# The third routing moved into the merged stage, and the second weights scaled by GpSimd in the second mixture

## The chip, the cores and the metric

The kernel runs on one core of one Trainium2 chip. The metric is the device time of one execution in microseconds, as the median of several runs. A profile of one execution (the trace) shows every instruction of the engines: TensorE (PE; its weight loads as PEld), VectorE (DVE), ScalarE (ACT), GpSimd (POOL) and the queue of SyncE (SP), which issues the DMAs.

## What is computed

`x` has 32 tiles of 128 tokens with 128 features; a context `ctx` has the same shape. Four layers follow each other, each of them a cross-attention onto the context and a feed-forward network, both added to `x` through a tanh gate. The networks are mixtures of 8 experts of which each token uses 2. What matters here is the network of the third layer and the attention of the fourth:

```python
# third network, N = 4096 tokens in all (the reference's shapes follow x)
capacity = int(1.2 * (N // E + 1))
logits = xf @ router_w.T + router_b
probs = softmax(logits)
top_vals, top_inds = top_k(probs, 2)
top_vals = top_vals / (sum(top_vals) + 1e-9)
e_flat, w_flat = top_inds.T.reshape(-1), top_vals.T.reshape(-1)     # all first choices, then all second ones
valid = w_flat > 1e-9
pos = cumsum(onehot(e_flat) & valid) - 1                            # place in the expert's queue
keep = valid & (pos_own < capacity)
h = gelu(toks @ fc1_w[e].T + fc1_b[e], approximate=False)           # 128 -> 512
y = toks + (h @ fc2_w[e].T + fc2_b[e]) * layer_scale[e]             # 512 -> 128
out[tok] += w * y
# attention of the fourth layer, 16 heads of 8: only the 32 largest scores of a row take part
cutoff = top_k(scores, 32)[0][..., -1:]
w = softmax(where(scores >= cutoff, scores, -inf))
```

## The kernel before

Every layer is a list of blocks. A block gives each engine its own instruction list; at its end all engines meet, and the next block begins. Inside, engines wait for each other by semaphores. For the third network and the fourth attention there are three blocks:

1. `normalise_measured("n2f")` normalises `x`, turns it into columns (`k.cols`) and multiplies by the router, the logits being copied out by VectorE (line 478).
2. `capacity_route("l2r")` (line 1808). SyncE fetches the router bias. VectorE runs one chain in which every instruction waits for the one before (`link`): softmax (the exponential on ScalarE, line 1847), `top_two`, the renormalised weights, the queue `queued`. TensorE counts the places with two matmuls, prefix and total (lines 1854 and 1855). VectorE goes on (line 1894 and after) until `k.weight` is written (line 1906).
3. `l3_attention` (line 2067), the merged stage: the fourth attention, whose tiles c = 0 to 31 run through TensorE, ScalarE, VectorE and GpSimd in a software pipeline, together with the experts of the third network, which run four tiles ahead. A step u of the experts handles a group of two token tiles (a token pair) and four of the eight experts, two steps per group. The order of the steps on each engine is a list given to `schedule`: each entry is a step and how far it lags; counter c runs from -4 (`AHEAD`). The steps that matter are, on TensorE, `hide` (first layer, line 2344, eight per u), `output` (second layer, line 2357, two parts x per u, both into the one PSUM bank `o2_ps`), `turn_weights` (2366) and `bias_rows` (2373); on ScalarE `gelu` (2455), `take_y` (2418, evicts a second-layer part and multiplies it by the token's weight), `take_weights`, `take_bias`; on GpSimd `stage_weights` (2236), `add_experts`, `add_base`; on VectorE `cutoffs` (2513 and 2515: the search for the 32nd largest score of each row, the largest work of the stage) and `measure`. Below, "step 0" and "step 1" are u = 0 and u = 1: the first two token tiles with experts 0 to 3, and with experts 4 to 7.

Before these steps VectorE scales the second-layer weights of the network by the layer scale, one expert at a time:

```python
for e in range(E):
    dve.tensor_tensor(w2[:, e, :, :], w2[:, e, :, :], per_group(scale_all[:, e, :], CHUNKS), ALU.mult
                      ).then_inc(scaled, 1)
```

The weights themselves (`k.l2f_w`) are fetched in the block `n1f`, ahead of the second mixture `l1_mixture` (line 1428), in which GpSimd only builds a small mask at the start.

## Time and profile before

| | before |
|---|---|
| median of 3 runs | 3255.04 us (3243.14 to 3259.41) |
| the profiled execution's own time | 3236.07 us |
| its span, first to last instruction | 3234.5 us |
| mean granted clock of TensorE | 0.91 |
| TensorE busy | 2863.1 us (89%) |
| VectorE busy | 2103.7 us (65%) |
| ScalarE busy | 1790.2 us (55%) |
| GpSimd busy | 1382.8 us (43%) |

Busy shares are means over the whole span; the routing in question takes place at about 1801 to 1827 us of it, the merged stage from 1827 on to about 2800, the second mixture from 880 to 1018. A granted clock of 1.00 is 2.4 GHz, 0.50 is 1.2 GHz. Durations in the timeline are those of an instruction or of a run of like instructions (x8); "idle before" says how long the engine stood and what it waited for.

### The profile page before, as it was taken

Reading aid. Unit: us, or ns where it says so; the run is one execution under the profiler, and the core shown is the slowest. Engines: PE = TensorE matmul, PEld = TensorE weight load, DVE = VectorE, ACT = ScalarE, POOL = GpSimd, SP = SyncE. Lnnn points to the kernel's source line nnn. Section 1 sums busy time; section 2 is a strip of 40 time slices with the busy share of each in tenths; the row PEclk is TensorE's granted clock in tenths of the full one; section 3 lists DMA queues with packets and bytes.
Section 4 is the critical chain, followed back from the end, with each engine's and each line's share of the span. In section 5 each row is a group of like instructions: output and inputs, shape, how many; then the busy total and the mean of one; then the engine's idle time right before and its main releaser. Section 6 shows DMA issues by size and latency. Waiting matters only on the chain. (4 is left out here: it accounts for less than half of the span.)

```text
span 3234.5 us, 68732 instructions
## 1 busy us (share of the span) xinstructions
PE 2863.1 (89%) x21380; PEld 2274.0 (70%) x21380; DVE 2103.7 (65%) x8010; ACT 1790.2 (55%) x5191; POOL 1382.8 (43%) x1680
## 2 busy tenths in 40 slices
PE   7999979957697999999999699999999986594998
PEld 5888844426554888888888577888888874484676
DVE  5444447747645555555555369999999998586332
ACT  5777734433222655555555368788878873251332
POOL 2222137737301333333333147777777776451000
PEclk9999989975598999999999899999999985696999
DMA  3000022323300000000000000000000000001000
GB/s 110 6 6 6 4 57 76 78 55 105 111 0 0 1 0 0 0 0 0 0 0 0 4 6 6 7 6 6 6 6 6 6 32 1 4 18 32 1 0 26
DMA packets 53771, 63.55 MB, mean 20 GB/s; under 512 B 5568, under 2 KB 37840, under 8 KB 53072
## 3 DMA queue, kind: packets, MB, share of 16 engines
q1 hardware_dynamic: 53600, 61.73, 6.6%
q8 instruction: 51, 0.84, 0.1%
q14 instruction: 120, 0.98, 0.1%
HBM read 57.19 MB, written 4.39 MB: 19 GB/s over the span
## 5 line engine op out<-in xcount | busy, mean ns | idle before, releaser
L1623 POOL TENSOR_TENSOR l2a_probs<-l2a_probs,l2a_inv 128x1024 f32<-128x1024 f32 x128 | 242.3, 1893 | 475.7 <-DVE l2a_inv L1789 475.7
L1734 ACT ACTIVATE l2a_probs<-l2a_s_ps,l2a_nm 128x256 f32<-128x256 f32 x512 | 237.2, 476 | 225.9 <-DVE l2a_nm L1765 225.9
L2513 DVE MAX8 l3a_top<-l3a_work 128x8 f32<-128x128 f32 x1536 | 314.0, 276 | 0.0
L2357 PEld LDWEIGHTS l3a_l2o_ps<-net_arena 128*128 128x128 f32 x2048 | 266.4, 214 | 65.7 <-issue 37.6
L2357 PE MATMUL l3a_l2o_ps<-net_arena 128*128 128x128 f32 x2048 | 278.2, 301 | 31.9 <-ACT net_l1f_gate L2418 29.3
L2219 POOL TENSOR_SCALAR l3a_above<-l3a_score,l3a_top 128x128 f32<-128x128 f32 x512 | 298.9, 602 | 16.4 <-DVE l3a_work L2515 7.5
L2515 DVE MATCH_REPLACE8 l3a_work<-l3a_top,l3a_work 128x128 f32<-128x128 f32 x1024 | 268.8, 274 | 0.0
L2344 PE MATMUL l3a_l2h_ps<-net_cols,net_arena 128*128 (+1 forms) x1024 | 248.2, 385 | 11.1 <-PEq L1830 7.6
L2455 ACT ACTIVATE net_arena<-l3a_l2h_ps,net_l2f_b 128x256 f32<-128x256 f32 x512 | 212.0, 486 | 37.8 <-PE l3a_l2h_ps L2344 34.9
L2344 PEld LDWEIGHTS l3a_l2h_ps<-net_cols,net_arena 128*128 128x128 f32 x1024 | 184.8, 191 | 60.4 <-issue 28.9
L698 ACT ACTIVATE l0a_probs<-l0a_score_ps,l0a_nm 128x128 f32<-128x128 f32 x512 | 180.0, 383 | 73.5 <-DVE l0a_nm L747 73.5
L2337 PEld LDWEIGHTS l3a_o_ps<-l3a_v,l3a_pT 128*128 128x128 f32 x1024 | 148.0, 216 | 73.7 <-ACT l3a_pT L2408 65.8
L2337 PE MATMUL l3a_o_ps<-l3a_v,l3a_pT 128*128 128x9 f32 x1024 | 147.7, 272 | 50.5 <-ACT l3a_pT L2408 50.5
L732 POOL TENSOR_TENSOR l0a_v<-l0a_v,l0a_inv 128x1024 f32<-128x1024 f32 x32 | 60.9, 1902 | 298.3 <-DVE l0a_inv L771 298.3
L2224 POOL TENSOR_TENSOR l3a_probs<-l3a_probs,l3a_above 128x512 f32<-128x512 f32 x128 | 162.8, 1272 | 54.6 <-ACT l3a_probs L2427 45.6
L1765 DVE TENSOR_REDUCE l2a_nm<-l2a_s_ps 128x2 f32<-128x512 f32 x256 | 159.0, 684 | 25.9 <-PE l2a_s_ps L1645 25.8
L2034 DVE SCALAR_TENSOR_TENSOR net_x<-l3f_o_ps,net_weight,net_x 128x128 f32 x256 | 72.7, 345 | 157.9 <-PE l3f_o_ps L1980 157.6
L2427 ACT ACTIVATE l3a_probs<-l3a_score,l3a_nm 128x128 f32<-128x128 f32 x512 | 159.5, 395 | 18.0 <-POOL l3a_nm L2203 17.7
L747 DVE TENSOR_REDUCE l0a_nm<-l0a_score_ps 128x4 f32<-128x512 f32 x128 | 82.2, 684 | 121.7 <-PE l0a_score_ps L658 121.7
L2014 ACT ACTIVATE l3f_hidden<-l3f_h_ps 128x512 f32<-128x512 f32 x130 | 77.5, 597 | 146.5 <-PE l3f_h_ps L1970 146.5
L1980 PEld LDWEIGHTS l3f_o_ps<-net_arena,l3f_hidden 128*128 128x128 f32 x1024 | 124.1, 192 | 30.9 <-issue 15.8
L1710 PE MATMUL l2a_side_ps<-net_arena,l2a_kv_t 128*128 128x256 f32 x512 | 144.4, 404 | 0.0
(523 smaller groups left out, 7171.6 us busy)
## 6 DMA issues: line engine op xcount, KB each, us to landing
l0f_code<-code_rows SPq DMA_DIRECT2D x32, 512.0 KB, 11.0
l1a_shift<-neg_top SPq DMA_DIRECT2D x16, 512.0 KB, 3.7
net_x<-x SPq DMA_DIRECT2D x4, 512.0 KB, 6.3
l0a_c_in<-ctxT SPq DMA_DIRECT2D x32, 64.0 KB, 1.8
net_arena<-L_w1T SPq DMA_DIRECT2D x1, 2048.0 KB
net_arena<-L_w2T SPq DMA_DIRECT2D x1, 2048.0 KB
l3a_k_in<-ctxT SPq DMA_DIRECT2D x32, 64.0 KB, 1.8
l3a_v_raw<-ctx SPq DMA_DIRECT2D x32, 64.0 KB, 2.0
```

The source lines that it names most:

```text
L698: act.activation(probs[c % 2][:, h, :], score[g][:, i * P:(i + 1) * P], ACT.Exp, bias=nm[:, h:h + 1], accum_out=sums[c % 2][:, h:h + 1]).t ...
L1623: pool.tensor_tensor(p[:, :, :], p[:, :, :], per_row(inv[c % 2][a][:, :, :].rearrange("p i o -> p (i o)"), KV), ALU.mult).then_inc(scaled, 1)
L1734: act.activation(probs[c % 2][a][:, 2 * i + odd, :], s_ps[a][odd][:, i * KV:(i + 1) * KV], ACT.Exp, bias=nm[c % 2][a][:, i, odd:odd + 1], ...
L2219: ins = pool.tensor_scalar(above[:, i, :], score[c % 4][:, h, :], top[c % 2][:, ROUNDS - 1, h, 7:8], None, ALU.is_ge)
L2224: pool.tensor_tensor(probs[c % 2][:, hs, :], probs[c % 2][:, hs, :], above[:, :, :], ALU.mult).then_inc(masked, 1)
L2337: ins = pe.matmul(o_ps[:, h, :], pT[n % 2][:, i, :], v[c % 4][:, h, :], start=True, stop=True)
L2344: ins = pe.matmul(h_ps[i][:, n * WIDE:(n + 1) * WIDE], w1[:, expert(u, x), 2 * i + n, :], k.cols[:, ds(group(q, u) * WIDE, WIDE)], start=T ...
L2357: ins = pe.matmul(o2_ps[:, at:at + D], hidden[2 * x + n][:, i, j * P:(j + 1) * P], w2[:, expert(u, 2 * x + n), i, :], start=(i == 0), stop ...
L2427: ins = act.activation(probs[c % 2][:, h, :], score[c % 4][:, h, :], ACT.Exp, bias=nm[c % 2][:, h:h + 1]).then_inc(probs_done, 1)
L2455: ins = act.activation(hidden[x][:, 2 * i + n, :], h_ps[i][:, n * WIDE:(n + 1) * WIDE], ACT.Gelu, bias=b1[:, e, 2 * i + n:2 * i + n + 1])
L2513: ins = dve.max(t[:, step // 2, h, :], src)
L2515: ins = dve.match_replace(work[:, h, :], t[:, step // 2, h, :], src, LOWEST)
```

## The change

The block `capacity_route("l2r")` is no longer called for this layer; its work is written into `l3_attention`. VectorE starts the merged stage with the routing chain, in tiles lent by the attention (`score[3]`, `score[2]`, `work`). ScalarE takes the exponential first. TensorE and ScalarE get a hand-written opening for u = 0 and 1 in place of the schedule's counters -4 and -3: first layers of u = 0, the two counting matmuls, both second-layer parts of u = 0 (the second one into the bank `s_ps[1]`, so that it does not wait for the eviction of the first), first layers of u = 1, then turned weights and bias rows; ScalarE evicts u = 0 only after the Gelus of u = 1. The schedule of both goes on at counter -2 (`first=2 - AHEAD`). The router bias becomes part of the weight fetch of `n1f`. The scaling of the second-layer weights and of `bias8` moves to GpSimd in `l1_mixture`, behind the mask and behind VectorE's scaling of that mixture's own weights. Inside the chain the epsilon is added in the same instruction as the sum, the two choices are handled in pairs without a wait between them, and the queue is written directly without copies.

```diff
@@ -218,6 +218,7 @@
     f.b1 = f.add(s.sb("l2f_b1", [P, E, 4])[:, :, :], d["L2_b1T"])
     f.scale8 = f.add(s.sb("l2f_scale8", [E, D])[:, :], d["L2_ffn_layer_scale"])
     f.bias8 = f.add(s.sb("l2f_bias8", [E, D])[:, :], d["L2_ffn_fc2_b"])
+    f.router_bias = f.add(s.sb("l2f_router_bias", [P, E])[:, :], d["L2_ffn_router_b"].partition_broadcast(P))
 
     f = k.l3a_w = Fetched(s, k, "l3a")
     f.wq = f.add(s.sb("l3a_wq", [P, P])[:, :], d["L3_WqT"])
@@ -1438,6 +1439,7 @@
         prod = [s.sb(f"prod{i}", [P, BANK]) for i in range(2)]
         hidden = s.sb("hidden", [P, NC, BANK])
         g_ps, u_ps, m_ps, y_ps = ([s.ps(f"{n}{i}", [P, BANK]) for i in range(2)] for n in ("g", "u", "m", "y"))
...
@@ -1452,6 +1454,14 @@
                 pool.affine_select(out=pair[:, :, :, :], in_=pair[:, :, :, :], compare_op=ALU.is_equal, fill=0.0,
                                    base=0, pattern=[[-2, E // 2], [-1, 2], [0, P // 2]], channel_multiplier=1
                                    ).then_inc(made, 1)
+                wn = k.l2f_w
+                pool.wait_ge(scaled, E)
+                wn.wait(pool)
+                for e in range(E):
+                    pool.tensor_tensor(wn.w2[:, e, :, :], wn.w2[:, e, :, :], per_group(wn.scale_all[:, e, :], 4), ALU.mult
+                                       ).then_inc(next_scaled, 1)
+                pool.tensor_tensor(wn.bias8[:, :], wn.bias8[:, :], wn.scale8[:, :], ALU.mult).then_inc(next_scaled, 1)
+                pool.wait_ge(next_scaled, E + 1)
 
             @block.tensor
             def _(pe):
@@ -2087,7 +2097,7 @@
         s = Space(nc, ctx, "l3a", k)
         w, wf = k.l3a_w, k.l2f_w
         wq, wk = w.wq, w.wk
-        w1, w2, b1, scale_all, scale8, bias8 = wf.w1, wf.w2, wf.b1, wf.scale_all, wf.scale8, wf.bias8
+        w1, w2, b1, bias8, router_bias = wf.w1, wf.w2, wf.b1, wf.bias8, wf.router_bias
         two = range(2)
         k_in = [s.sb(f"k_in{i}", [P, P]) for i in two]
         v_raw = [s.sb(f"v_raw{i}", [P, D]) for i in two]
@@ -2115,19 +2125,37 @@
             "dif", "both", "spread", "mean", "rstd", "shift"))
         normed = s.sb("normed", [P, GT, D])
 
...
+        NE, LQ = NB * E, 2 * NB
+        p, rest, eq = (spare(score[3], i * NE, NB, E) for i in range(3))
+        sel = [spare(score[3], (3 + i) * NE, NB, E) for i in two]
+        best = [spare(score[3], 5 * NE + i * NB, NB) for i in two]
+        red = spare(score[3], 5 * NE + 2 * NB, NB)
+        queued, carry, total, until = (spare(work, 2 * i * NE, *shape) for i, shape in enumerate((
+            (2, NB, E), (E, LQ), (E, LQ), (E, LQ))))
+        place = spare(score[2], 0, E, LQ)
+        capacity = int(1.2 * (NB * P // E + 1))
+
         ov_ps, p_ps, o2_ps, misc_ps = (s.ps(n, [P, BANK]) for n in ("o", "p", "l2o", "misc"))
         s_ps = [s.ps(f"s{i}", [P, BANK]) for i in two]
         h_ps = [s.ps(f"l2h{i}", [P, BANK]) for i in two]
         q_ps = s_ps[1][:, 0:P]
+        prefix_ps, total_ps, early_ps = p_ps, ov_ps, s_ps[1]
         o_ps = ov_ps[:, 0:H * (DA + 1)].rearrange("p (h d) -> p h d", h=H)
...
@@ -2138,14 +2166,14 @@
             if not isinstance(q, int) or n >= 1:
                 eng.wait_ge(sem, n)
 
-        def schedule(eng, steps, loops=LOOPS):
+        def schedule(eng, steps, loops=LOOPS, first=-AHEAD):
 
             def run(q, c):
                 for step, behind in steps:
                     if not isinstance(q, int) or 0 <= q * BODY + c - behind < NB:
                         step(q, c - behind)
 
-            for c in range(-AHEAD, FIRST):
+            for c in range(first, FIRST):
                 run(0, c)
             if loops:
                 with eng.Fori(0, loops) as q:
@@ -2169,6 +2197,9 @@
         def in_group(step, at):
 
             return lambda q, u: step(q, u // GT) if u % GT == at else None
+
+        def output_bank(u, x):
+            return early_ps if (u, x) == (0, 1) else o2_ps
 
         def for_part(step, n):
 
@@ -2193,6 +2224,9 @@
 
             @block.gpsimd
             def _(pool):
+                pool.memset(carry[:, :, :], 1.0).then_inc(carry_made, 1)
+                pool.wait_ge(carry_made, 1)
+                pool.memset(carry[:, :, 0:1], 0.0).then_inc(carry_made, 1)
                 for t in v:
                     pool.memset(t[:, :, :], 1.0).then_inc(filled, 1)
                 pool.wait_ge(filled, 4)
@@ -2233,6 +2267,8 @@
                 def stage_weights(q, g):
                     wait(pool, y_ready, q, PARTS, GT * PARTS * (g - 1))
                     wait(pool, wT_mm, q, GROUP, g - 1)
+                    if g == 0:
+                        pool.wait_ge(routed, 1)
                     pool.tensor_copy(w_stage[g % 2][:, :, :], k.weight[:, ds(first_tile(q, g), GT), :]).then_inc(w_staged, 1)
 
                 def add_experts(q, u):
@@ -2347,14 +2383,13 @@
 
                 def output(q, u, x):
                     wait(pe, act_done, q, 2 * EX, 2 * EX * u + EX * (x + 1))
-                    wait(pe, y_ready, q, PARTS, PARTS * u + x)
-                    if isinstance(q, int) and u < GT:
-                        pe.wait_ge(scaled, E + 1)
+                    if (u, x) != (0, 1):
+                        wait(pe, y_ready, q, PARTS, PARTS * u + x)
                     for n in two:
                         for j in range(GT):
                             at = (n * GT + j) * D
                             for i in range(CHUNKS):
-                                ins = pe.matmul(o2_ps[:, at:at + D], hidden[2 * x + n][:, i, j * P:(j + 1) * P],
+                                ins = pe.matmul(output_bank(u, x)[:, at:at + D], hidden[2 * x + n][:, i, j * P:(j + 1) * P],
                                                 w2[:, expert(u, 2 * x + n), i, :], start=(i == 0), stop=(i == CHUNKS - 1))
                     ins.then_inc(o_mm, 1)
 
@@ -2382,6 +2417,19 @@
                     for j in range(GT):
                         ins = pe.transpose(misc_ps[:, j * P:(j + 1) * P], normed[:, j, :], k.ident[:, :])
                     ins.then_inc(turned, 1)
+
+                for at in range(2 * EX):
+                    hide(0, 0, at)
+                pe.wait_ge(queue_ready, 2)
+                flat = queued.rearrange("p i t e -> p (i t e)")
+                pe.matmul(prefix_ps[:, :], k.upto[:, :], flat, start=True, stop=True).then_inc(counted, 1)
+                pe.matmul(total_ps[:, :], k.ones[:, :], flat, start=True, stop=True).then_inc(counted, 1)
+                output(0, 0, 0)
+                output(0, 0, 1)
+                for at in range(2 * EX):
+                    hide(0, 1, at)
+                turn_weights(0, 0)
+                bias_rows(0, 0)
...
+                              (for_part(apply, 3), 2), (for_part(scores, 2), -1)], first=2 - AHEAD)
 
             @block.scalar
             def _(act):
                 w.wait(act)
                 wf.wait(act)
+                act.wait_ge(shifted, 1)
+                act.activation(p, p, ACT.Exp).then_inc(exped, 1)
 
                 def take_cols(q, g):
                     wait(act, turned, q, GROUP, g + 1)
@@ -2415,7 +2465,7 @@
                         wait(act, w_staged, q, GROUP, u // GT + 1)
                     for n in range(2 * GT):
                         e = expert(u, 2 * x + n // GT)
-                        ins = act.activation(y[x][:, n, :], o2_ps[:, n * D:(n + 1) * D], ACT.Copy,
+                        ins = act.activation(y[x][:, n, :], output_bank(u, x)[:, n * D:(n + 1) * D], ACT.Copy,
                                              scale=w_stage[u // GT % 2][:, n % GT, e:e + 1])
                     ins.then_inc(y_ready, 1)
 
@@ -2475,6 +2525,14 @@
                         ins = act.activation(normed[:, j, :], xt, ACT.Identity, scale=rstd[:, j:j + 1],
                                              bias=shift[:, j:j + 1])
                     ins.then_inc(norm_done, 1)
+
+                for u in two:
+                    for at in range(2 * EX):
+                        gelu(0, u, at)
+                take_y(0, 0, 0)
+                take_y(0, 0, 1)
+                take_weights(0, 0)
+                take_bias(0, 0)
...
+                               (for_part(take_p, 3), 2), (in_group(take_weights, 0), -AHEAD), (for_part(take_scores, 2), -1)], first=2 - AHEAD)
 
             @block.vector
             def _(dve):
                 w.wait(dve)
                 wf.wait(dve)
-                for e in range(E):
-                    dve.tensor_tensor(w2[:, e, :, :], w2[:, e, :, :], per_group(scale_all[:, e, :], CHUNKS), ALU.mult
-                                      ).then_inc(scaled, 1)
-                dve.tensor_tensor(bias8[:, :], bias8[:, :], scale8[:, :], ALU.mult).then_inc(scaled, 1)
+                link = Chain(dve, chain)
+                link(dve.tensor_tensor(k.logits[:, :, :], k.logits[:, :, :], per_group(router_bias, NB), ALU.add))
+                link(dve.tensor_reduce(red, k.logits[:, :, :], AX.X, ALU.max))
+                dve.tensor_tensor(p, k.logits[:, :, :], per_row(red, E), ALU.subtract).then_inc(shifted, 1)
+                dve.wait_ge(exped, 1)
+                link(dve.tensor_reduce(red, p, AX.X, ALU.add))
+                link(dve.reciprocal(red, red))
+                link(dve.tensor_tensor(p, p, per_row(red, E), ALU.mult))
+                top_two(link, dve, k, p, rest, eq, red, best, sel)
+                link(dve.scalar_tensor_tensor(out=red, in0=best[0], scalar=1e-9, in1=best[1], op0=ALU.add, op1=ALU.add))
+                link(dve.reciprocal(red, red))
+                chosen = rest[:, :, 0:2].rearrange("p t i -> p i t")
+                for i in two:
+                    dve.tensor_tensor(best[i], best[i], red, ALU.mult).then_inc(chain, 1)
+                link.n += 2
+                dve.wait_ge(chain, link.n)
+                for i in two:
+                    dve.tensor_scalar(chosen[:, i, :], best[i], 1e-9, None, ALU.is_gt).then_inc(chain, 1)
+                link.n += 2
+                dve.wait_ge(chain, link.n)
+                for i in two:
+                    dve.tensor_tensor(queued[:, i, :, :], sel[i], per_row(chosen[:, i, :], E), ALU.mult).then_inc(queue_ready, 1)
+                dve.wait_ge(counted, 2)
+                dve.wait_ge(carry_made, 2)
+
+                def by_expert(ps):
+                    return ps[:, :].rearrange("p (l e) -> p e l", e=E)
+                link(dve.tensor_copy(total, by_expert(total_ps)))
+                link(dve.tensor_tensor_scan(until.rearrange("p e l -> p (e l)"), carry.rearrange("p e l -> p (e l)"),
+                                            total.rearrange("p e l -> p (e l)"), 0.0, ALU.mult, ALU.add))
+                link(dve.tensor_tensor(until, until, total, ALU.subtract))
+                link(dve.tensor_tensor(place, by_expert(prefix_ps), until, ALU.add))
+                link(dve.tensor_scalar(place, place, float(capacity), None, ALU.is_le))
+                for i in two:
+                    kept = place[:, :, i * NB:(i + 1) * NB].rearrange("p e t -> p t e")
+                    dve.tensor_tensor(sel[i], queued[:, i, :, :], kept, ALU.mult).then_inc(chain, 1)
+                link.n += 2
+                dve.wait_ge(chain, link.n)
+                for i in two:
+                    dve.tensor_tensor(sel[i], sel[i], per_row(best[i], E), ALU.mult).then_inc(chain, 1)
+                link.n += 2
+                dve.wait_ge(chain, link.n)
+                link(dve.tensor_tensor(sel[0], sel[0], sel[1], ALU.add))
+                dve.tensor_scalar(k.weight[:, :, :], sel[0], k.tg[:, 6:7], None, ALU.mult).then_inc(routed, 1)
+                dve.wait_ge(routed, 1)
                 dve.tensor_reduce(w_sum[:, :], k.weight[:, :, :], AX.X, ALU.add).then_inc(summed, 1)
 
                 def cutoffs(q, c, half):
@@ -2836,8 +2935,6 @@
                      l1_route(nc, k), l1_mixture(nc, k)),
             lambda: l2_cross(nc, k),
             lambda: (normalise_measured(nc, k, "n2f", keep_rows=True, gate_w=k.gates_w[:, 2, :], logits=k.logits),
-                     capacity_route(nc, k, "l2r", k.tg[:, 6:7], int(1.2 * (NB * P // E + 1)), True,
-                                    bias=k.d["L2_ffn_router_b"], floor=1e-9, add_eps=1e-9),
                      l3_attention(nc, k)),
             lambda: l3_block(nc, k),
         ]
```

## Rows read from the trace of the kernel before

**Rows 1.** Windows: span, then busy us (instructions) per engine, clock, DMA share, GB/s.

```profile
1801.00:1827.10 26.10, 3.78 (x4) 1.17 (x4) 16.62 (x40) 0.42 (x1) 0.78 (x3) 0.57 0.00 0
1827.10:1890.80 63.70, 57.66 (x342) 47.51 (x343) 5.93 (x13) 35.85 (x96) 15.64 (x33) 0.98 0.03 7
1890.80:2640.00 749.20, 704.79 (x4585) 605.96 (x4584) 721.75 (x4592) 600.32 (x1513) 571.17 (x936) 0.94 0.02 6
```

**Rows 2.** Timeline of the routing block: start, duration, engine, line, operation, [idle before].

```profile
1800.56 0.29 DVE L478 COPY net_logits<-n2f_logit_ps 128x128 f32<-128x128 f32 x1 [4.98 <-PE n2f_logit_ps L497]
...
1804.22 0.42 DVE L1862 TENSOR_TENSOR net_logits<-net_logits,l2r_router_bias 128x256 f32<-128x256 f32 x1 [3.38 <-DMA l2r_router_bias<-L_ffn_router_b]
...
1805.59 0.42 ACT L1847 ACTIVATE l2r_p<-l2r_p 128x256 f32<-128x256 f32 x1 [6.66 <-DVE l2r_p L1865]
...
1812.38 0.19 DVE L1871 TENSOR_TENSOR l2r_red<-l2r_best 128x32 f32<-128x32 f32 x1
...
1815.03 0.62 DVE L1885 COPY l2r_queued<-l2r_sel 128x256 f32<-128x256 f32 x2
...
1826.11 0.35 DVE L1906 TENSOR_SCALAR net_weight<-l2r_sel,net_tg 128x256 f32<-128x256 f32 x1
```

**Rows 3.** Timeline of the opening of the merged stage.

```profile
1827.12 3.06 PEld L2344 LDWEIGHTS l3a_l2h_ps<-net_cols,net_arena 128*128 128x128 f32 x8 [9.16 <-issue]
...
1829.30 1.28 ACT L2455 ACT_TABLE_LOAD   x1 [23.30 <-PE l3a_l2h_ps L2344]
1830.60 1.57 ACT L2455 ACTIVATE net_arena<-l3a_l2h_ps,net_l2f_b 128x256 f32<-128x256 f32 x4
...
1836.78 1.70 ACT L2455 ACTIVATE net_arena<-l3a_l2h_ps,net_l2f_b 128x256 f32<-128x256 f32 x4 [0.36 <-PE l3a_l2h_ps L2344]
...
1837.66 3.74 PE L2357 MATMUL l3a_l2o_ps<-net_arena 128*128 128x128 f32 x32
1838.37 0.36 ACT L2462 ACTIVATE l3a_l2wT<-l3a_misc_ps 8x256 f32<-8x256 f32 x1
...
1846.32 3.95 PE L2344 MATMUL l3a_l2h_ps<-net_cols,net_arena 128*128 128x256 f32 x16
1847.39 1.70 ACT L2455 ACTIVATE net_arena<-l3a_l2h_ps,net_l2f_b 128x256 f32<-128x256 f32 x4 [4.81 <-PE l3a_l2h_ps L2344]
...
1848.98 1.14 ACT L2418 ACTIVATE net_l1f_up<-l3a_l2o_ps,l3a_l2w_stage 128x128 f32<-128x128 f32 x4
...
1854.89 0.71 PE L2373 MATMUL l3a_misc_ps<-net_l2f_bias,l3a_l2wT 8*128 8x128 f32 x4
...
1855.53 3.84 PE L2357 MATMUL l3a_l2o_ps<-net_arena 128*128 128x128 f32 x32
...
1890.76 1.65 DVE L2513 MAX8 l3a_top<-l3a_score 128x8 f32<-128x128 f32 x8 [20.48 <-ACT l3a_score L2445]
```

**Rows 4.** Waits of VectorE from 1890 to 2640 us: total, times, longest.

```profile
DVE l3a_inv L2522 <- PE l3a_o_ps L2337: 26.0, 20, 2.5
```

**Rows 5.** Windows: the counting matmuls, and second layers of step 0.

```profile
1815.70:1819.60 3.90, 3.78 (x4) 1.17 (x4) 0.02 (x1) 0.00 (x0) 0.00 (x0) 0.50 0.00 0
...
1835.00:1840.00 5.00, 4.94 (x34) 4.12 (x33) 0.00 (x0) 3.32 (x9) 0.00 (x0) 1.00 0.00 0
```

**Rows 6.** Timeline of TensorE in the second mixture.

```profile
902.31 1.02 PE L1472 MATMUL l1f_g_ps<-net_cols,net_l1f_gate 128*128 x2
903.17 1.02 PE L1473 MATMUL l1f_u_ps<-net_cols,net_l1f_up 128*128 x2
```

**Rows 7.** One line: durations min/median/max ns of the masking product on GpSimd.

```profile
L2224 POOL TENSOR_TENSOR l3a_probs<-l3a_probs,l3a_above x128: 1263/1272/1283, 1921.9 to 2750.7; 128x512 f32<-128x512 f32 x128
```

**Rows 8.** Windows: the second mixture up to its end.

```profile
900.00:1018.00 118.00, 110.10 (x471) 59.79 (x469) 56.45 (x103) 24.75 (x38) 0.00 (x0) 1.00 0.00 0
```

**Rows 9.** The page's costliest groups, two of the second attention: busy, mean ns.

```profile
L1623 POOL TENSOR_TENSOR l2a_probs<-l2a_probs,l2a_inv 128x1024 f32<-128x1024 f32 x128 | 242.3, 1893 | 475.7 <-DVE l2a_inv L1789 475.7
...
L1765 DVE TENSOR_REDUCE l2a_nm<-l2a_s_ps 128x2 f32<-128x512 f32 x256 | 159.0, 684 | 25.9 <-PE l2a_s_ps L1645 25.8
```

More of the change, by code:

```diff
@@ L2116, in l3_attention, with spare @@
         normed = s.sb("normed", [P, GT, D])
+        def spare(tile, start, *shape):
+            flat = tile[:, :, :].rearrange("p h s -> p (h s)")[:, start:start + int(np.prod(shape))]
+            names = "abc"[:len(shape)]
+            return flat if len(shape) == 1 else flat.rearrange(f"p ({' '.join(names)}) -> p {' '.join(names)}",
+                                                               **dict(zip(names, shape)))
+        NE, LQ = NB * E, 2 * NB
[7 more added lines that the diff above has]
+        capacity = int(1.2 * (NB * P // E + 1))
         ov_ps, p_ps, o2_ps, misc_ps = (s.ps(n, [P, BANK]) for n in ("o", "p", "l2o", "misc"))
@@ L2393, in _ @@
                               (for_part(apply, 2), 2), (for_part(turn_probs, 3), 2), (in_group(turn_weights, 0), -AHEAD),
-                              (for_part(apply, 3), 2), (for_part(scores, 2), -1)])
+                              (for_part(apply, 3), 2), (for_part(scores, 2), -1)], first=2 - AHEAD)
             @block.scalar
```

8 lines of the change are left out of this document (5 added, 3 removed).

## The prediction

> **What bounds the kernel now.** I read the page first (its shares stand in the table above). TensorE is busy for 89% of the span, but that is a mean over stages that wait for each other at block boundaries, so I cut out the stretch around the third routing by windows [rows 1]. The routing block with its boundaries lasts 26.1 us (1801.0 to 1827.1), in which TensorE works for 3.78 us and VectorE for 16.62: a serial chain on one engine with everything else standing. Then come 63.7 us of the merged stage in which VectorE works for 5.93 us and TensorE for 57.66: VectorE's search for the 32nd largest score can't start before the first scores, and these stand in TensorE's queue behind the third network's expert steps 0 to 3. From 1890.8 on VectorE is busy 721.75 of 749.20 us and TensorE 704.79.
>
> The timeline of the routing [rows 2] shows the chain: last logits copied at 1800.85 (1800.56 + 0.29), a wait for the router bias until 1804.22, one instruction after another up to the queue's copies, which end at 1815.65, two counting matmuls, and again one chain until the weights at 1826.46. The timeline of the opening of the merged stage [rows 3] shows what comes then: TensorE loads for the first layers of step 0 at 1827.12, their Gelus run from 1830.60 to 1838.48, second layers start at 1837.66, first layers of step 1 at 1846.32, bias rows at 1854.89, second layers of step 1 at 1855.53. That last instruction is my mark: from it on the instructions of every engine keep their order in the change, so by whatever it is early, the first search at 1890.76 is early, and all behind it.
>
> **Which of two engines paces the long part?** In the waits of VectorE there [rows 4] one kind recurs: 20 waits for attention outputs of TensorE, 26.0 us in total. So both engines are nearly full, and both have their whole queue behind the mark. A shift of the mark moves both.
>
> **The routing block goes.** The merged stage starts behind the normalisation's last copy. The boundary at the end of the routing took 0.66 us (1826.46 to 1827.12), so I let the stage start at 1801.51. The bias comes with the earlier weight fetch: 1804.22 - 1801.51 = 2.71 us of waiting goes at once.
>
> **VectorE's chain to the queue.** From the bias add to the first sum of the two probabilities nothing changes: 1812.38 - 1804.22 = 8.16 us. From there to the end of the copies (1815.65) it took 3.27 us; TensorE's idle window closes at 1815.7 [rows 5], so with the handing over it is 3.38 us. The two copies (0.62) go, the added epsilon is fused (an instruction of this size, 0.19, and its start: 0.22), and three pairs run without a wait between their halves, which saves something between 0 and the rest of half of their time, 0.9; I take 0.44. That leaves 3.38 - 0.62 - 0.22 - 0.44 = 2.10. The counting can start at 1801.51 + 8.16 + 2.10 = 1811.77.
>
> **The first layers in the meantime.** ScalarE now has the exponential ahead of its Gelus. It ends 1.79 us after the chain's start (1804.22 to 1806.01), at 1803.30; the Gelu table takes 1.28; Gelus need 7.88 us (1830.60 to 1838.48) and end at about 1812.5. TensorE's first layers were all issued 10.54 us after its first load (1827.12 to 1837.66), now by 1812.0 at the latest (a transpose of weights stood in between and moves away). So the counting starts at 1811.8, and routing chain and first layers take the same 10.3 us side by side. This is the whole point: 26 us of routing shrink to what is left of them behind the first layers.
>
> **The counting matmuls.** Before they took 3.78 us at a granted clock of 0.50, that is 1.2 GHz, TensorE having been idle from 1801 on [rows 1, 5]. Two matmul pairs of the same shape at 1.00, in the second mixture, start at 902.31 and are through at 904.19: 1.88 us [rows 6]. In the changed kernel TensorE has just done eight first layers; in the stretch that corresponds, 1835 to 1840, the clock was 1.00. I take 1.88 (end 1813.65) and keep 3.78 as the bound.
>
> **Second layers of step 0, first layers of step 1.** The load row of a second-layer part lasts 3.65 us, and the next starts behind it. The second part has a bank of its own and no longer waits for ScalarE, so the first layers of step 1 begin at 1813.65 + 7.30 = 1820.95. The first Gelu follows 1.07 later (1846.32 to 1847.39), and eight groups without an eviction in between take 7.88: end at 1829.90. The evictions of step 0, moved behind all Gelus, now lie on the path: two of 1.14, then the turned weights 0.36, then on TensorE the bias rows 0.64. Together 3.28, with 0.1 for handing over: the mark at 1833.3. Before it was 1855.53. Gain 22.2 us.
>
> **The rest of the routing.** Behind the counts VectorE needed about 6.9 us (1819.6 to 1826.46): weights at 1820.6. GpSimd waits for them before it stages them; queued behind this wait are its additions of the experts, and TensorE's turned weights and ScalarE's evictions wait for the staging. They want it at 1829, so 8 us cover the whole tail; without that cover it would cost its lateness one for one. VectorE's sum of the weights behind it is wanted only after the evictions.
>
> **The scaling.** On VectorE it was over before anything waited: all of that engine's work before 1890.8 is 5.93 us [rows 1], and second layers began 10.5 us into the stage behind the Gelus. So nothing is saved by taking it away. On GpSimd I take the 128x512 product of two SBUF tiles, 1.27 us [rows 7]: eight, and as much again for the small ninth at most, 11.4 us, in a stage in which GpSimd is idle from 900 to 1018 and the DMA share 0.00, the weights having landed [rows 8]. With GpSimd done by 912 the block's end at 1018 is untouched. The price would come by VectorE, if GpSimd held it up: at most 11.4 us. In the second attention, where GpSimd multiplies for 1893 ns at a time, VectorE's reduction of 512 columns from PSUM has a mean of 684 ns [rows 9], 1.34 ns a column, not more than the 1.64 of the routing's 256 columns in 0.42 us with GpSimd idle [rows 2]; the mixture's products also read one side from PSUM. I take zero. The Trainium skill ("SBUF — State Buffer", section "Who interferes with whom") says that a VectorE instruction with two SBUF inputs and a GpSimd one that reads SBUF shut each other out, and that one with a single SBUF input doesn't take part. By that rule the mixture's products stay free and zero stands; were they both from SBUF, the sum would be the first rival's.
>
> **Sum.** The profiled execution spanned 3234.5 and took 3236.07 us; less 22.2 that is 3213.9. The median of the runs shown is 3255.04, 19 above it, so the prediction is 3255.04 - 22.2 = 3232.8, rounded to 3233.
>
> **Bounds of the sum.** Counting at half clock costs 1.9, pairs that save nothing 0.4, a second table load 1.28: gain 18.6. Pairs that save all give 0.5 more: 22.7. So 3232 to 3236 by the terms, if nothing else happens.
>
> **Rivals.**
> *GpSimd holds VectorE up in the second mixture.* Full price 11.4 us, gain 10.8, time 3244. For it: the two never ran together in that stage. Against it: [rows 9]. Chance 0.05.
> *The head start is lost in the long part.* VectorE waits for TensorE 20 times there [rows 4]; if that part is held by something that doesn't move with the mark, the gain shrinks to 0 to 12 us, time about 3249. Against it: the only things not behind the mark are the first loads, issued by the stage's own start. Chance 0.08.
> *Slower.* The long part falls into another rhythm between TensorE's and ScalarE's queues. It runs 749.2 us over about 29 of the 32 tiles. The gain is used up from 22.2/29 = 0.77 us per tile on, and the kernel is slower by over 0.5% (16 us) from 1.3 us per tile. VectorE's mean wait is now 0.9 per tile, so it would have to more than double; with 1.5 us more per tile the time is 3276. For it: with TensorE at 94% a small slip is not made good. Against it: order and distances behind the mark are as before. Chance 0.04.
> *The forecast,* 18 to 24 us gained: 0.83.
>
> **From cases to numbers.** A change under 0.5%, 16 us, can't be told from none here: the three runs span 16 us. The forecast's 22 us lie only 6 above it, so I give it a seventh for landing inside, 0.12; with the first two rivals "same" gets 0.25, faster 0.71, slower 0.04. The range adds the scatter of medians (about 10 us each way) to 3232 to 3236, and 4 for a true centre of the runs below their median; it takes in the first rival: 3218 to 3247.
>
> **What the profile would show.** Right: no idle TensorE between normalisation and merged stage, both counting matmuls 10.3 us after the stage's start in about 1.9 us, the mark 32.4 us and the first search 67.7 us behind the normalisation's last copy, eight GpSimd products of about 1.27 us in the second mixture with VectorE's own unchanged. Wrong: longer VectorE products in the mixture, the mark over 36 us behind the copy, GpSimd's staging behind 28, or a longer period per tile afterwards.

## The result and the profile after

The changed kernel takes 3232.99 us (median of 8, 3219.45 to 3239.96) against 3255.1 (8, 3243.14 to 3259.93) for the kernel before on the same chip: ratio 0.993, interval 0.991 to 0.9949, 22.1 us less. The change ran in two more comparisons: 0.996 (0.9941 to 0.9979) and 0.9929 (0.9908 to 0.995). None of the three intervals reaches 1, so it is faster, by less than 1%: 22.1, 15.5 and 20.5 us.

Its profiled execution took 3219.45 us and spanned 3217.7, only 16.8 less than before. The timeline below shows the merged stage's opening, last logits copy first (columns as in [rows 2]). Times are compared from the end of that copy on, written "behind the copy" or with a plus sign below; it ends at 1805.36 here and at 1800.85 before.

```profile
1805.07 0.29 DVE L479 COPY net_logits<-n2f_logit_ps 128x128 f32<-128x128 f32 x1 [4.98 <-PE n2f_logit_ps L498]
...
1805.75 0.43 DVE L2552 TENSOR_TENSOR net_logits<-net_logits,net_l2f_router_bias 128x256 f32<-128x256 f32 x1 [0.39 <-PEq L439]
...
1805.83 3.75 PE L2380 MATMUL l3a_l2h_ps<-net_cols,net_arena 128*128 128x256 f32 x8 [0.80 <-PEq L439]
...
1807.21 0.42 ACT L2449 ACTIVATE l3a_score<-l3a_score 128x256 f32<-128x256 f32 x1 [3.76 <-DVE l3a_score L2554]
1807.64 1.28 ACT L2505 ACT_TABLE_LOAD   x1
...
1813.99 0.19 DVE L2560 SCALAR_TENSOR_TENSOR l3a_score<-l3a_score 128x32 f32<-128x32 f32 x1
...
1815.24 0.76 DVE L2572 TENSOR_TENSOR l3a_work<-l3a_score 128x256 f32<-128x256 f32 x2
1815.56 1.70 ACT L2505 ACTIVATE net_arena<-l3a_l2h_ps,net_l2f_b 128x256 f32<-128x256 f32 x4 [0.36 <-PE l3a_l2h_ps L2380]
...
1816.22 1.02 PE L2425 MATMUL l3a_p_ps<-l3a_work,net_upto 128*128 128x512 f32 x2
...
1817.08 1.02 PE L2426 MATMUL l3a_o_ps<-l3a_work,net_ones 128*128 128x512 f32 x2
...
1817.94 3.73 PE L2392 MATMUL l3a_l2o_ps<-net_arena 128*128 128x128 f32 x32
...
1821.51 3.74 PE L2392 MATMUL l3a_s_ps<-net_arena 128*128 128x128 f32 x32
...
1824.45 0.35 DVE L2594 TENSOR_SCALAR net_weight<-l3a_score,net_tg 128x256 f32<-128x256 f32 x1
...
1824.94 0.20 POOL L2272 COPY l3a_l2w_stage<-net_weight 128x16 f32<-128x16 f32 x1 [18.00 <-DVE net_weight L2594]
...
1825.08 8.07 PE L2380 MATMUL l3a_l2h_ps<-net_cols,net_arena 128*128 128x256 f32 x32
...
1832.33 1.70 ACT L2505 ACTIVATE net_arena<-l3a_l2h_ps,net_l2f_b 128x256 f32<-128x256 f32 x4 [0.36 <-PE l3a_l2h_ps L2380]
...
1832.99 0.38 PE L2401 MATMUL l3a_misc_ps<-net_ident,l3a_l2w_stage 128*8 128x128 f32 x2
1833.92 1.14 ACT L2468 ACTIVATE net_l1f_gate<-l3a_l2o_ps,l3a_l2w_stage 128x128 f32<-128x128 f32 x4
1834.92 1.17 ACT L2468 ACTIVATE net_l1f_up<-l3a_s_ps,l3a_l2w_stage 128x128 f32<-128x128 f32 x4
...
1835.91 0.36 ACT L2512 ACTIVATE l3a_l2wT<-l3a_misc_ps 8x256 f32<-8x256 f32 x1
...
1836.32 0.71 PE L2408 MATMUL l3a_misc_ps<-net_l2f_bias,l3a_l2wT 8*128 8x128 f32 x4 [2.95 <-ACT l3a_l2wT L2512]
```

TensorE then, in a view of that engine alone (the mark), and VectorE's first search:

```profile
1836.96 5.47 PE L2392 MATMUL l3a_l2o_ps<-net_arena 128*128 128x128 f32 x32
```
```profile
1873.84 1.26 DVE L2612 MAX8 l3a_top<-l3a_score 128x8 f32<-128x128 f32 x6 [20.47 <-ACT l3a_score L2495]
```

Read against [rows 2, 3]: routing chain and first layers run side by side, the counting starts at 1816.22, and GpSimd stages the weights at 1824.94, 8 us before TensorE wants them (1832.99). From the last Gelu's end (1834.03) to the mark the steps follow one another: evictions, turned weights, bias rows. TensorE stands for 2.95 us of it. Behind the copy the mark lies at 31.60 us (before 54.68) and the first search at 68.48 (before 89.91).

Windows of the same stretches (columns as in [rows 1]):

```profile
1805.80:1808.00 2.20, 2.17 (x5) 1.84 (x6) 1.56 (x4) 0.77 (x2) 1.09 (x6) 0.50 0.18 49
1816.00:1818.00 2.00, 2.00 (x7) 0.99 (x6) 0.00 (x0) 1.23 (x4) 0.00 (x0) 1.00 0.00 0
1825.00:1837.00 12.00, 8.86 (x42) 6.21 (x40) 0.25 (x1) 8.94 (x25) 1.72 (x4) 1.00 0.00 1
1837.00:1845.00 8.00, 6.68 (x44) 6.52 (x44) 0.00 (x0) 1.52 (x5) 4.53 (x7) 0.79 0.01 2
1873.80:2623.00 749.20, 703.40 (x4588) 604.72 (x4587) 721.29 (x4590) 600.31 (x1515) 571.47 (x937) 0.94 0.02 6
900.00:1018.00 118.00, 111.17 (x470) 59.91 (x469) 56.23 (x101) 25.34 (x39) 0.00 (x0) 1.00 0.00 0
```

The clock is 0.50 at the stage's start, 1.00 (2.4 GHz) at the counting matmuls, and 0.79 on average behind the mark: the pause ahead of the bias rows is followed by a dip. The last two rows stand against [rows 1, 8]: the long part is as full as before, and so is the second mixture.

**Where the other microseconds of the span went.** The first normalisation with a router (n0f) ends 5.9 us later than before (431.0 against 425.1), at a place that the change doesn't touch. Windows of it, after and then before:

```profile
411.00:413.00 2.00, 0.63 (x4) 0.42 (x4) 1.50 (x7) 1.67 (x5) 2.00 (x3) 1.00 0.00 0
...
415.00:417.00 2.00, 2.00 (x12) 2.00 (x11) 1.59 (x7) 1.91 (x5) 0.86 (x1) 0.50 0.00 0
...
419.00:425.00 6.00, 6.00 (x31) 6.00 (x31) 0.29 (x1) 3.08 (x7) 0.00 (x0) 0.50 0.00 0
425.00:431.00 6.00, 5.99 (x30) 5.89 (x28) 0.00 (x0) 1.19 (x2) 0.00 (x0) 0.50 0.01 3
```
```profile
412.00:414.00 2.00, 0.50 (x4) 0.42 (x4) 1.31 (x7) 1.52 (x4) 2.00 (x3) 1.00 0.00 0
414.00:416.00 2.00, 1.86 (x17) 1.60 (x16) 1.59 (x8) 1.96 (x6) 2.00 (x2) 1.00 0.00 0
416.00:418.00 2.00, 2.00 (x22) 2.00 (x20) 1.59 (x8) 2.00 (x7) 1.05 (x1) 1.00 0.00 0
```

From 415 or 416 on TensorE is busy all the time in both, but at 1.2 GHz in one and 2.4 GHz in the other. The two logits copies of n0f and of n2f lie 5.3 us apart at full clock and 9.0 at half. Of the twelve traces of this study ten have n0f at half clock, two edits of the kernel before among them, and five have n2f; the profiled execution of before is the only one with n0f, n1f and n2f all at full clock. So this isn't the change's. At n2f's last copy 4.5 us of it are left (1805.36 against 1800.85), and the 21.1 us gained at the merged stage's end less 4.5 make 16.6 of the span's 16.8. (Here and below, the end of the merged stage is read at one fixed instruction, 3.2 us into the next stage, where VectorE has the first group of its statistics.)

### The profile page after: what moved, and what is told of

Same layout as the page of the kernel before. It is cut to its first block and busy times, and to the rows that moved or that the text cites. A ratio compares the mean times of both kernels' runs of the same rounds, so it can differ in the third digit from the quotient of the medians.

```text
span 3217.7 us, 68717 instructions
## 1 busy us (share of the span) xinstructions
PE 2868.6 (89%) x21380; PEld 2280.0 (71%) x21380; DVE 2095.8 (65%) x7998; ACT 1789.0 (56%) x5191; POOL 1392.2 (43%) x1689
```

## Experiments

Kernels are compared behind the end of n2f's last logits copy, which leaves that scatter out.

**The change again**, nothing edited, to see which numbers repeat.

> The changed kernel unchanged, for a second trace of it and a ratio on the chip of the other runs. Theory: the first trace lost two things. In the normalisation ahead of the second half of layer one (n0f) it fell to half clock and took 7.2 us longer than before; if that belongs to the single execution, the second trace has about 17 us there again or not, independently of the change. At second layers of step 1 (the mark) TensorE had stood 3 us for the moved evictions and then worked at half clock, 5.47 us instead of 3.84; if that is a consequence of the new order, it is there again. Expected: mark 31.6 us behind the last logits copy, first search 68.3 to 68.5 behind it (before: 89.9), ratio to before 0.993. Rival, both are chance: the mark's second-layer part takes 3.8 us here and the first search comes at 66.8.

Measured: 3237.85 us, ratio 0.996. The mark lies at +31.59, the search at +68.47, the counting at +10.85, and the second layers at the mark take 5.47 us again: all the same to 0.1 us, while the span was 3224.4, 6.7 longer. A third trace of the change (below, beside another version) has them at +31.64 and +68.54, with 5.46 us. So the opening repeats and the rest scatters.

**The scaling alone**, in the kernel before:

```diff
@@ second mixture, GpSimd
+                wn = k.l2f_w
+                pool.wait_ge(scaled, E)
+                wn.wait(pool)
+                for e in range(E):
+                    pool.tensor_tensor(wn.w2[:, e, :, :], ...).then_inc(next_scaled, 1)
@@ merged stage, VectorE
-                for e in range(E):
-                    dve.tensor_tensor(w2[:, e, :, :], ...).then_inc(scaled, 1)
... (the same for bias8; TensorE no longer waits for `scaled`)
```

> The kernel before with only the scaling of the second weights moved to GpSimd in the second mixture, routing block as before. Theory: worth nothing, neither in the mixture (its products on VectorE stay at 0.69 us, the stage lasts the same) nor in the merged stage (second layers of step 0 start about 10.5 us behind its first load as before). Ratio 1.000 within 0.2%. Rival, GpSimd holds VectorE up in the mixture: up to 11 us more, ratio 1.003. Rival, the scaling was on the path before: 1 to 5 us less, ratio 0.999.

Measured: 3257.67 us, ratio 1.0007 (0.9988 to 1.0026). GpSimd's products in its trace, and VectorE's first product of the mixture, in this run and then before:

```profile
L1460 POOL TENSOR_TENSOR net_arena<-net_arena x8: 1264/1265/1268, 888.0 to 896.6; 128x512 f32<-128x512 f32 x8
...
892.48 0.69 DVE L1528 TENSOR_TENSOR l1f_prod<-l1f_u_ps,l1f_gate 128x512 f32<-128x512 f32 x1 [4.59 <-PE l1f_u_ps L1482]
```
```profile
888.06 0.69 DVE L1519 TENSOR_TENSOR l1f_prod<-l1f_u_ps,l1f_gate 128x512 f32<-128x512 f32 x1 [4.56 <-PE l1f_u_ps L1473]
```

Zero, as costed. The interval alone leaves room for 6 us either way; the trace is sharper. VectorE's products keep their 0.69 us beside GpSimd's, the mixture lasts 137.9 us from its first VectorE instruction to that of the next stage (138.0 before), and the first search comes 89.95 us behind the copy (89.91 before).

**The scaling beside the routing**: the changed kernel, but GpSimd scales at the opening of the merged stage, and TensorE's second layers wait for it.

```diff
@@ merged stage, GpSimd
+                wf.wait(pool)
+                for e in range(E):
+                    pool.tensor_tensor(w2[:, e, :, :], ...).then_inc(next_scaled, 1)
... (the same for bias8; both are gone from the second mixture)
@@ merged stage, TensorE, behind the counting matmuls
+                pe.wait_ge(next_scaled, E + 1)
                 output(0, 0, 0)
```

> The changed kernel, but GpSimd scales the second weights at the start of the merged stage, beside VectorE's routing chain, instead of in the mixture. Theory (the Trainium skill, SBUF - State Buffer, Who interferes with whom: a VectorE instruction with two SBUF inputs and a GpSimd instruction that reads SBUF exclude each other): VectorE's products of 128x256, 0.42 us alone, wait for GpSimd's of 1.27 us, and the queue is ready 3 to 8 us later than 10.4 us after the stage's start; the mark and the time follow by the same 3 to 8 us. Rival, the engines don't disturb each other: GpSimd is done 12 us after the stage's start, just when the second layers begin, and mark and time are those of the changed kernel within 1 us.

Measured: 3238.97 us, ratio 0.9946 (0.9931 to 0.9961); the mark at +38.34, 6.7 us later than in the change. The timeline of VectorE in its routing chain, of GpSimd and of TensorE, and a window of the counting:

```profile
1810.16 0.42 DVE L793 TENSOR_REDUCE l3a_score<-l3a_score 128x32 f32<-128x256 f32 x1
1810.61 0.92 DVE L794 TENSOR_TENSOR l3a_score<-l3a_score 128x256 f32<-128x256 f32 x1
1811.57 1.38 DVE L795 TENSOR_TENSOR l3a_score<-l3a_score,net_rank 128x256 f32<-128x256 f32 x1
...
1819.07 0.43 DVE L797 TENSOR_TENSOR l3a_score<-l3a_score 128x256 f32<-128x256 f32 x1
...
1820.79 0.76 DVE L2570 TENSOR_TENSOR l3a_work<-l3a_score 128x256 f32<-128x256 f32 x2
```
```profile
1807.35 10.94 POOL L2227 TENSOR_TENSOR net_arena<-net_arena 128x512 f32<-128x512 f32 x8
...
1821.60 2.08 PE L2422 MATMUL l3a_p_ps<-l3a_work,net_upto 128*128 128x512 f32 x2 [4.86 <-DVE l3a_work L2570]
...
1823.47 1.68 PE L2423 MATMUL l3a_o_ps<-l3a_work,net_ones 128*128 128x512 f32 x2
```
```profile
1821.60:1825.10 3.50, 3.50 (x6) 1.62 (x6) 0.00 (x0) 0.00 (x0) 0.00 (x0) 0.54 0.00 0
```

The chain needs 15.47 us to the queue (1806.08 to 1821.55) in place of 10.25, because single instructions grow: those with two inputs in SBUF take 0.92 to 1.38 us in place of 0.42, the reductions between them, with one input, stay at 0.42, and behind GpSimd's last product (1818.29) all are back at 0.42. The later queue then meets a TensorE that has stood for 4.86 us, and the counting runs at a clock of 0.54: it takes 3.55 us in place of 1.88. The later start of the counting (5.1 us) and this 1.7 make the 6.7. The Trainium skill ("SBUF — State Buffer", section "Who interferes with whom") says that a port pair shared by VectorE and GpSimd is an exclusive lock, that a VectorE instruction with two SBUF inputs contends there with a GpSimd instruction that reads SBUF, and that one with a single SBUF input, outside the modes that use both ports, doesn't. The trace agrees on which instructions grow and which don't. So it matters where the scaling goes: it costs nothing in a mixture whose products read PSUM, and 6.7 us at the mark here. At the stage's end the delay is still there (+961.3, the change's three traces +951.3 to +954.1). The medians are too coarse for it: 3238.97 stands against 3237.85 for the change on the same chip and 3232.99 in its first comparison.

**A filler in the pause ahead of the bias rows**, in the changed kernel, so that TensorE doesn't stand:

```diff
                 turn_weights(0, 0)
+                for _ in range(24):
+                    pe.transpose(p_ps[:, 0:P], k.ident[:, :], k.ident[:, :])
                 bias_rows(0, 0)
```

> The changed kernel with 24 transposes of the identity on TensorE between the turned weights and the bias rows, the place where it stands 3 us for the moved evictions (2.8 us of work in a gap of 2.95 us; results go to a bank that nobody reads). Theory, the half clock at the mark comes from that standing: the second-layer part of step 1 takes 3.8 instead of 5.47 us and the first search comes 1.5 us earlier behind the last logits copy (66.8 instead of 68.4). Rival, the fall of the clock comes from the low work of TensorE beforehand (four first-layer pairs in 8.1 us) or from chance: the part takes over 5 us all the same.

Measured: 3232.92 us, ratio 0.993 (0.9905 to 0.9954). The timeline of TensorE, and a window behind its mark:

```profile
1846.97 0.71 PE L2408 MATMUL l3a_misc_ps<-net_l2f_bias,l3a_l2wT 8*128 8x128 f32 x4 [0.34 <-ACT l3a_l2wT L2514]
1847.61 3.84 PE L2392 MATMUL l3a_l2o_ps<-net_arena 128*128 128x128 f32 x32
```
```profile
1847.60:1856.00 8.40, 7.08 (x62) 6.90 (x62) 0.00 (x0) 1.53 (x5) 4.84 (x7) 1.00 0.00 0
```

The mark stays (+31.56), the part at it takes 3.84 us in place of 5.47 at a clock of 1.00, and the search comes at +66.83 in place of 68.48. The pause costs 1.6 us of clock besides its own length. It isn't chance: the part takes 5.46 or 5.47 us in all four traces in which TensorE stands there (three of the change, and the scaling beside the routing), and 3.73 to 3.84 in all eight in which it doesn't. In time nothing can be read: 3232.92 lies among the change's own medians, 3231.35 to 3237.85.

**Evictions ahead of the last Gelus**, in the changed kernel, against the 2.9 us that they cost on the path (ScalarE's edit told in words):

```diff
@@ TensorE, behind output(0, 0, 1)
-                for at in range(2 * EX):
-                    hide(0, 1, at)
                 turn_weights(0, 0)
+                hide(0, 1, 0)
+                hide(0, 1, 1)
                 bias_rows(0, 0)
+                for at in range(2, 2 * EX):
+                    hide(0, 1, at)
@@ ScalarE: take_y(0, 0, 0) and take_weights behind gelu(0, 0, ...), take_y(0, 0, 1) and take_bias behind gelu(0, 1, 1)
```

> The changed kernel with another order in the hand-written opening: ScalarE evicts the first part of step 0 before the Gelus of step 1 and the second part after the first two of them; TensorE turns the weights straight behind the second layers of step 0 and does the bias rows behind the first two first-layer parts of step 1. Theory: the 3.3 us of evictions and turned weights leave the path, for some 1.2 to 1.7 us put between the Gelus; TensorE doesn't stand for 3 us, so the second layers of step 1 run at full clock. Mark 1.5 to 2.5 us earlier (29 to 30 us behind the last logits copy instead of 31.6), its part 3.8 us, first search at 64.5 to 65.5 instead of 68.4. In time 3 to 4 us less than the changed kernel, ratio to before about 0.992. Rival: waiting for the staged weights (19.6 us behind the copy) and the insertions cost as much as they free, mark at 31 to 32; then only the clock is won, 1.6 us, first search at 66.8.

Measured: 3225.97 us, ratio 0.9912 (0.9896 to 0.9928); the mark at +28.80, its part 3.73 us, the search at +63.97, 4.5 ahead of the change. But its stage ended 954.3 us behind the copy, the change's 951.3. So the lead was gone by the end, and it was open whether the 7 us in the time were scatter. Two runs repeated it, the second with a longer warm-up of TensorE in the normalisations (WARM = 38 in place of 24), against their half clock.

> The version with the earlier evictions once more, for a second trace and as the base of the run beside it. Theory: mark 28.8 us and first search 64.0 us behind the last logits copy again; the stretch from the first search to the end of the merged stage, 890.4 us in its first trace and 882.5 to 887.7 in the others, falls back among the others (883 to 888), as that stretch scatters with the granted clock. Rival: the new order in the opening costs the long part 3 to 5 us for good, and it is 890 again.

> The same with 38 instead of 24 idle transposes ahead of each of the three normalisations that feed a router, so that TensorE is busy until the first rows are normalised (2.8 us now, then 1.8 us idle). Theory: these blocks sometimes fall to half clock, which costs 7.2 us each (last logits copy of n0f 23 us behind its start instead of 16); if the idle stretch brings that about, it becomes rarer, n0f comes at full clock, and the time is 3 to 10 us less than that of the version beside it. Rival: the fall comes while the block works (its transposes and 8-column matmuls), the extra transposes change nothing, n0f stays at half clock and the times are equal within 0.2%.

Measured: 3225.23 us, 0.9916 (0.9882 to 0.9949), and 3224.0, 0.9913 (0.9878 to 0.9947). The opening repeats: marks at +28.77 and +28.87, searches at +63.94 and +64.02. The longer warm-up changes nothing in the time that the intervals could show. In its trace it shortens TensorE's stand ahead of n0f's first rows from 1.80 to 0.28 us, and the clock falls all the same, only later:

```profile
415.00:417.00 2.00, 2.00 (x20) 2.00 (x20) 0.58 (x3) 2.00 (x6) 0.00 (x0) 1.00 0.00 0
417.00:419.00 2.00, 2.00 (x13) 2.00 (x13) 0.29 (x1) 1.99 (x6) 0.00 (x0) 0.52 0.00 0
```

TensorE had worked there since 410.81 at a clock of 1.00 and went on without a gap at 0.50. n0f's last copy starts 19.8 us behind the first warm-up transpose, against 23.3 in the change's first trace, at half clock, and 16.2 in the run beside it, in which n0f ran at full clock and n2f didn't. So the stand just ahead isn't what brings the fall about, or not alone. Then both versions together on one chip:

> The changed kernel, beside the version with earlier evictions on the same chip. In the traces so far the merged stage of the changed kernel ended 951.3 and 953.9 us behind the last logits copy (972.4 before), that of the version with earlier evictions 954.4, 952.4 and 952.9, although its first search began 4.5 us earlier; the medians of earlier calls, 3233 to 3238 against 3225 to 3226, say otherwise. Theory A, the lead is lost in the long part, which TensorE paces at a clock that scatters: the two medians differ by less than 3 us. Theory B, the lead arrives: this one 4 to 8 us longer than the other. Ratio to before 0.993 to 0.996 in both.

> The version with earlier evictions, beside the changed kernel on the same chip. Theory A: median within 3 us of the changed kernel's, ratio to before 0.993 to 0.995; end of the merged stage 952 to 955 us behind the last logits copy. Theory B: 4 to 8 us less than the changed kernel, ratio 0.991 to 0.992, end of the merged stage at 947 to 951.

Measured: 3231.35 us, 0.9929 (0.9908 to 0.995), and 3230.68, 0.993 (0.9907 to 0.9953): 0.7 us apart. From the first search to the end of the stage the traces show 882.8, 885.4 and 885.5 us for the change, and 890.4, 888.5, 888.8 and 886.5 for this version: 4.5 us ahead at the search, 4.0 longer behind it on average. The stage ends at +951.3, +953.9 and +954.1 in the change and at +954.3, +952.4, +952.9 and +950.5 in this version. In the pair on one chip that is 954.1 against 950.5, so 3.6 us of the lead arrive there, as theory B has it, while the two times are as theory A has them. VectorE's waits in the long part, of the first trace of each:

```profile
DVE l3a_inv L2621 <- PE l3a_o_ps L2373: 26.5, 20, 2.1
```
```profile
DVE l3a_inv L2626 <- PE l3a_o_ps L2373: 33.7, 23, 3.3
```

VectorE waits 7.2 us more for attention outputs in this pair, the widest one. In all traces, from the first search up to 830 us behind the copy, it is 26.5, 28.6 and 28.8 us in the change and 33.7, 32.2, 32.7 and 29.7 here, 4.1 more on average. The reciprocals of these outputs begin, for tiles 0, 2, 4, 6, 7, 9 and 11, 143.9, 196.5, 249.1, 303.5, 329.8, 383.7 and 438.2 us behind the copy in the change's first trace and 139.4, 191.0, 244.9, 300.4, 328.4, 383.0 and 437.8 in this version's: a lead of 4.2 to 5.5, then 3.1, 1.4, 0.7, 0.4. In the pair on one chip the lead is 4.6 at tile 0 and still 2.3 at tile 11.

**The router bias alone**, fetched earlier, in the kernel before:

```diff
-                    sp.dma_start(router_bias[:, :], bias.partition_broadcast(P)).then_inc(w_in, 16)
@@ routing block, VectorE
-                    dve.wait_ge(w_in, 16)
+                    k.l2f_w.wait(dve)
@@ the weight fetch of `n1f`
+    f.router_bias = f.add(s.sb("l2f_router_bias", [P, E])[:, :], d["L2_ffn_router_b"].partition_broadcast(P))
```

> The kernel before with only the router bias fetched with the weights instead of at the start of the routing block. Theory: the wait of 2.7 us at the head of the chain goes and everything behind it moves: routing's first instruction 0.4 to 0.7 us behind the last logits copy instead of 3.4, second layers of step 1 at 51.9 us behind it instead of 54.7. Rival: another wait takes its place, mark at 54 or later.

Measured, in one execution of 3244.15 us, too few for a ratio: the counting starts at +11.85 us and the first layers at +23.25, 3.1 ahead of before, but the mark comes at +53.82 and the search at +89.05, 0.9 ahead only. That is neither the 51.9 of the theory nor another wait. TensorE's timeline and clock at the opening of its merged stage:

```profile
1828.50 3.75 PE L2340 MATMUL l3a_l2h_ps<-net_cols,net_arena 128*128 128x256 f32 x8 [7.61 <-PEq L1831]
...
1832.84 7.44 PE L2340 MATMUL l3a_l2h_ps<-net_cols,net_arena 128*128 128x256 f32 x20 [0.59 <-ACT net_arena L2451]
```
```profile
1832.00:1842.00 10.00, 9.35 (x35) 7.21 (x35) 1.85 (x5) 6.53 (x17) 0.00 (x0) 0.70 0.01 2
```

The clock rose later than before: it was 0.50 up to 1838, 9.5 us into the stage, where before had 1.00 from 1831 on, 4 us into it. So the 24 instructions after the first eight take 8.31 us in place of 6.12. Of 3.1 us saved 2.2 went to the clock in this execution; whether it would be so in every one isn't shown.

## Why the prediction was right

**Boundary and bias.** Predicted: start 0.66 us behind the copy, and no wait for the bias. It was 0.39: right, and 0.3 less. TensorE starts at 1805.83, having stood for 0.80 us at the boundary.

**Chain to the queue.** 8.16 + 2.10 = 10.26 us predicted up to the start of the counting, 10.47 measured (1805.75 to 1816.22): the part that doesn't change took 8.24, and the handing over to TensorE 0.22 where 0.11 stood. The pairs took 0.29, 0.28 and 0.76 us, together 1.40 with their starts in place of 1.82, so the 0.44 taken from between the bounds held.

**Counting at full clock.** 1.88 predicted and 1.88 measured (1816.22 to 1818.10), clock 1.00. I read this as the work of the first layers right ahead of it giving the clock: where TensorE had to stand for 4.86 us, in the scaling beside the routing, it took 3.55 us (1821.60 to 1825.15), near the bound of 3.78.

**Second bank, first layers of step 1.** Predicted at 1820.95, that is 20.1 behind the copy; measured 19.7 (1825.08). The two second-layer parts take 6.98 us and not 7.30. No run takes the second bank out, so its worth is read from this timeline alone.

**Evictions on the path.** 3.28 and 0.1 of handing over predicted, 2.93 measured from the last Gelu to the mark; the two evictions, listed as 1.14 and 1.17, start only 1.00 apart. The version with evictions earlier takes 2.8 us off the mark, so they do lie on the path.

**The rest of the routing** is hidden: weights at 19.4 us, staged at 19.6, wanted by TensorE's transposes at 27.6: a cover of 8.0, as predicted.

**Sum to the mark.** 32.4 predicted, 31.60 measured: 23.1 us gained there, 0.9 more than predicted. At the first search it is 21.4 (68.48 where 67.7 was predicted), since the part at the mark took 5.47 us and not the 3.84 of before. **This is the step that I missed.** I listed the 3.3 us of evictions as a length only, and didn't ask what TensorE does meanwhile: it stands, and its clock falls. The filler showed this: same mark, 1.65 us earlier search. Two errors of opposite sign, 0.9 and 1.6 us, left the gain near 22; that they nearly cancel is luck.

**Scaling.** Zero predicted, zero in the second mixture, where VectorE's products from PSUM keep their length, and 1.0007 for the edit alone. The first rival's mechanism exists: where VectorE's inputs both lie in SBUF the products hold it up.

**The long part.** The forecast was that the head start passes through. For this change it does: the attention outputs come 21.5 us earlier behind the copy in the first tile (165.4 to 143.9), 20.4 in the third (216.9 to 196.5), 20.2 to 20.5 up to the 25th and about 21.1 in the last ones, and the stage's end 21.1 (972.4 to 951.3). This part scatters by itself: from the first search on it lasts 882.5, 885.0 and 886.8 us in the traces of the kernel before and of the two edits of it (the scaling alone, the bias alone), and 882.8, 885.4 and 885.5 in those of the change. But the reason, "both engines have their whole queue behind the mark", doesn't cover everything. Of the 4.5 us that the earlier evictions add, 4.0 are gone at the stage's end on average over four traces against three, and VectorE waits 4.1 us longer for TensorE; in one pair 3.6 arrived. Of the filler's 1.7 us nothing is seen at the end (954.5 us, the change's 951.3, 953.9 and 954.1), but one trace in such a scatter can't say that they are lost. I read this as TensorE pacing that part; the runs show the loss on average and the waits, and no more. The rival "the head start is lost" is true of most of that extra lead and not of the change. Why this is so in detail, TensorE's short dips of clock or the order of its queue against ScalarE's, wasn't told apart. Nor is it excluded that the earlier evictions gain a few microseconds: their ratios measured apart from the change, 0.9912, 0.9916 and 0.9913, are below its 0.993 and 0.996; side by side the two are equal, with intervals of 0.2% each way.

**Medians.** The difference of medians is 22.1 us where 22.2 stood, and the median is 3233 as predicted. The three comparisons, 15.5 to 22.1, say that hitting it to a microsecond was luck. The single trace would have said 16.8.

## What to carry to other kernels

A serial chain on one engine between two stages can be hidden behind the next stage's work that doesn't need its result; the price, here, is the evictions and waits that the reordering puts on the path. Ask of each such wait not only how long TensorE stands but what its clock does behind it: here 3 us of standing cost 1.6 us more. And compare kernels behind an event just ahead of the edit: the first pair of whole spans held 4.5 us from code that the edit doesn't touch.

## What was not expected of the hardware

- TensorE's clock can fall to 1.2 GHz and stay there while the engine is busy without a gap: n0f from 415 to 431 us, 2.00 of 2.00 us busy, transposes and 8-column matmuls, after a window with 0.63 busy of 2.00 us. Before, 0.50 of 2.00 was followed by 1.00. With the longer warm-up the engine stood for only 0.28 us, worked for 6 us at 1.00 and then fell to 0.50 in the midst of the same work. What decides it stays open.
- GpSimd's 128x512 products took 1.27 us each in the mixture and mostly 1.44 beside the chain, while VectorE's two-input instructions went from 0.42 to up to 1.38.
